# An attention and expert-layer kernel on one core: one wait of SyncE removed, three weight loads and two statistics steps moved in the order

## The chip, the cores and the metric

The kernel runs on one core of one Trainium2 chip. The metric is the device time of one execution in microseconds (us). The time before is the median of three runs.

## The reference, cut to what matters

```
x = x + xattn(layernorm(x), ctx, mask, mask, Wq, bq, Wk, bk, Wv, bv)   # 8 batches of 256 x 512, 16 heads
n = layernorm(x)                                                      # the last axis, 512 long
shared = (sigmoid(flat @ shared_gate.T) * (flat @ shared_up.T)) @ shared_down.T   # flat: 2048 rows of n
comb   = the two largest of softmax(flat @ router_w.T) over 8 experts, 0 elsewhere
he     = sigmoid(flat_bf16 @ w_gate[e].T) * (flat_bf16 @ w_up[e].T)               # 352 wide
routed = sum over e of comb[:, e] * (he @ w_down[e].T)
x = x + (n + shared + routed)
```

The change touches the passage from the attention part to the expert part: the end of the attention sum, the second layernorm, the shared gate and up products, and the loads of the expert weights.

## The kernel before, in words

Each of the five engines has a queue of its own (`Queue`, line 42). Every piece of work is put there with a number, its place, by `pe.at`, `act.at`, `dve.at`, `pool.at` or `sp.at`, and the queue is sorted by that number. So the numbers set only the order of the work of one engine. What one engine needs from another is a semaphore wait inside the piece, and everything behind a waiting piece on the same engine waits too. Two units of place matter: `base` is 17.0, where the attention units end, and `dt_` is 1/32, one step of the list `seq` (line 1179) of the shared part.

**The attention.** 16 units (two per batch) of 8 heads each are worked through. At the end of a unit `finish_unit` (line 1098) divides the result by the sums of the softmax: SyncE (SP) writes the reciprocals to DRAM (line 1128), reads them back spread over the partitions into `RB` (`gather_back`, line 1135, semaphore `rb`), and GpSimd (POOL) multiplies and adds to X (`add`, lines 1143 and 1144, semaphore `a`). The last unit is u = 15.

**The second layernorm.** It is done for four blocks of 512 rows: `norm(8)` to `norm(11)` (line 399). The statistics of the last block, `norm(11)`, are on VectorE (DVE): `first_three` (line 403) takes three of the four tiles and is placed 2.9 steps ahead of `stage_a` (line 420), which takes the fourth tile (line 429, it waits for `a` = 16) and closes the sums (line 431). `stage_p` (line 434, lines 440 to 449, nine small operations) turns them into scale and offset on POOL. ScalarE (ACT, `normalise`, line 482) then writes two normalised tiles of the block and DVE (`other_half`, line 492) the other two, both into Y[1].

**The shared products.** TensorE (PE) follows `seq`: ("T", blk, j) transposes half of a block (line 1259), ("G", blk, it) makes one third of gate and up (24 matmuls and more, line 1303), ("R", blk) turns the router's columns (line 1372), C and I work out and invert the places of the routed rows. T of block 3 waits for the two normalised halves (`xn` = 12 and `xd`). After each T, ACT or DVE takes the upper half of the number (line 1279) and DVE the lower one (`rest`, line 1284). After each G there is a chain ACT `tanh` (line 1325), DVE `hidden` (line 1338), ACT `upper` (line 1355), POOL `lower` (line 1360, semaphore `h`). From the third G on, `tanh` waits until `lower` of the G two places earlier is done.

**The normalised rows.** POOL writes a bf16 copy of each block (`narrow`, line 1621), and SP stores it to DRAM (`store_rows`, line 1629) into `yr`, from which the experts' rows are gathered later (line 1699, issued by POOL). The stores of blocks 0 and 2 count on `s_yr[0]`, those of blocks 1 and 3 on `s_yr[1]`. The store of block 0 first waits for `rb` = 256, the landing of the last `gather_back`.

**The expert weights.** 1088 KB for each of 8 experts go by POOL's own DMA queue into BIG (`load_expert`, line 332, the DMA at line 334). Their order and their waits are in `early_expert` (line 1658). Expert 0 is loaded early. Experts 1 and 2 stand at 16.95 and 16.951. Experts 7, 6 and 5 stand at `when(("G", 1, 2)) + .91 * dt_`, which is between `stage_p` of norm(11) (.90) and `lower` of G(1, 2) (.92). All three wait for the end of the attention (`av`), expert 7 also for `fr0` and `fr1`, and expert 5 also for `s_yr[1]` = 16, the landing of the store of block 1, because it overwrites the copy that this store reads. The first expert product (line 1764) waits for all eight.

The order on POOL before, at the place in question: `add` of unit 15; loads of experts 1 and 2; `lower` of G(0, 2); `stage_p` of norm(11); loads of experts 7, 6 and 5; `lower` of G(1, 2); `narrow` of block 2. The order on DVE before: `hidden` of G(0, 2); `first_three`; `hidden` of G(1, 2); `rest` of T(2, 0); `stage_a`; `rest` of T(2, 1); `hidden` of G(0, 0); `other_half`.

Of the kernel before, what the change touches and what calls it, by code (L numbers as in the profile page):

```python
# [14 lines left out]
T = 512  # L15
NU = 16
# [51 lines left out]
def xattn_moe(nc, x, ctx, mask, maskc, wqkv, bqk, bv, sg, su, sd, we, out):  # L68
# [10 lines left out]
    with stack:  # L79
# [170 lines left out]
        pe, act, dve, pool, sp = (Queue() for _ in range(5))  # L250
# [81 lines left out]
        def load_expert(i):  # L332
            def emit(e):
                e.dma_start(BIG[:, i, :], we[i]).then_inc(s["we"], 16)
            return emit
# [861 lines left out]
        base, dt_ = 17.0, 1 / 32  # L1197
# [9 lines left out]
        def when(item):  # L1207
            if item in early:
                return 15.15 + .22 * early.index(item)
            if item in last:  # L1210
                n = last.index(item)
                return tb + BETWEEN[n] + 1.7 if n < nb else tb + NP + 2.1 + n * 2.5
            if item == ("R", 3):
                return base + (seq.index(item) + 1.2) * dt_
            if item == ("C",):
                return base + (seq.index(item) + 1.5) * dt_
            return base + seq.index(item) * dt_
# [405 lines left out]

        def store_rows(blk):
            def f(e):
                if blk == 0:
                    e.wait_ge(s["rb"], 16 * NU)
                e.wait_ge(s["yb"], blk + 1)
                e.dma_start(yr[512 * blk:512 * blk + 512].rearrange("(a p) t -> p a t", p=128), YBF[blk])\
                    .then_inc(s_yr[blk % 2], 16)  # L1630
            return f
# [15 lines left out]
        norm(8, 13.2, 13.3, (13.66, 13.85, 14.1, 14.3), (6.7, 7.7, 8.7, 9.7))  # L1647
        norm(9, 13.8, 13.85, (14.52, 14.68, 14.85, 15.02), (10.7, 11.18, 12.18, 13.18))
        norm(10, 15.04, 15.06, 15.72, (11.68, 12.68, 13.68, 15.02))
        norm(11, when(("T", 2, 1)) + .55 * dt_, when(("G", 1, 2)) + .9 * dt_, when(("G", 0, 0)) + .85 * dt_)  # L1650
        rows_at = (15.06, 15.4, when(("T", 2, 1)) + .9 * dt_, when(("T", 3, 1)) + .9 * dt_)
        for blk in range(4):
            pool.at(rows_at[blk], narrow(blk))
# [4 lines left out]
        def early_expert(i):  # L1658
            def f(e):

                if i == 0:
                    e.wait_ge(s_nl[1], 32 * 16)
                elif i <= 2:
                    e.wait_ge(s["rp"], zi["x", 31, 3, 1] + 1)
                if i == 7:
                    e.wait_ge(s["fr0"], NU)
                    e.wait_ge(s["fr1"], NU)
                if i == 3:
                    e.wait_ge(s["rc"], zi["k", 15, 1] + 1)
                    e.wait_ge(s["gu"], max(gi[q] for q in gi if q[1] == 1) + 1)  # L1670
                if i == 4:
                    e.wait_ge(s["gu"], max(gi[q] for q in gi if q[1] == 0) + 1)
                if i == 5:
                    e.wait_ge(s_yr[1], 16)
                if i >= 5:
                    e.wait_ge(s["av"], 4 * NG)
                load_expert(i)(e)
            return f
        pool.at(15.6, early_expert(0))
        for n, i in enumerate((1, 2, 7, 6, 5)):  # L1680
            pool.at(16.95 + n / 1000 if n < 2 else when(("G", 1, 2)) + (.91 + n / 1000) * dt_, early_expert(i))
        pool.at(when(("G", 3, 2)) + .3 * dt_, early_expert(4))
        pool.at(when(("G", 2, 0)) + .3 * dt_, early_expert(3))

# [300 lines left out]
```

## Time and profile before

| what | value |
|---|---|
| three runs | 655.5, 657.47, 662.83 us |
| median | 657.47 us |
| the profiled execution: its time | 655.5 us |
| the profiled execution: its span, first to last instruction | 653.6 us |
| mean granted TensorE clock, as a share of the full one | 0.995 |
| busy: PE, DVE, ACT, POOL | 606.2, 506.8, 472.1, 364.1 us |

The time is longer than the span by what lies around the instructions. A row of a timeline gives start, length, engine, line and operation; brackets at its end give the idle time of the engine before it and what ended that. SPq is SyncE's queue of DMA issues. A busy DMA share of 1.00 means that all 16 DMA engines of the core work.

### The profile page before, as it was taken

Reading aid. Unit: us, or ns where it says so; the run is one execution under the profiler, and the core shown is the slowest. Engines: PE = TensorE matmul, PEld = TensorE weight load, DVE = VectorE, ACT = ScalarE, POOL = GpSimd, SP = SyncE. Lnnn points to the kernel's source line nnn. Section 1 sums busy time; section 2 is a strip of 40 time slices with the busy share of each in tenths; the row PEclk is TensorE's granted clock in tenths of the full one; section 3 lists DMA queues with packets and bytes.
Section 4 is the critical chain, followed back from the end, with each engine's and each line's share of the span. In section 5 each row is a group of like instructions: output and inputs, shape, how many; then the busy total and the mean of one; then the engine's idle time right before and its main releaser. Section 6 shows DMA issues by size and latency. Waiting matters only on the chain.

```text
span 653.6 us, 12535 instructions
## 1 busy us (share of the span) xinstructions
PE 606.2 (93%) x4082; PEld 258.5 (40%) x4082; DVE 506.8 (78%) x982; ACT 472.1 (72%) x662; POOL 364.1 (56%) x497
## 2 busy tenths in 40 slices
PE   4799989999999999999999999889999889999987
PEld 4544333333333333333333232224554456666532
DVE  2489899999999999999999999855447634454577
ACT  3654999899899899899898879984432266667511
POOL 5558554684684684684684463051642577777510
PEclk9799999999999999999999999999999999999999
DMA  8642334544536436444343342124797323333278
GB/s 290 209 135 84 94 119 142 144 136 145 144 99 184 140 102 194 127 148 135 108 120 121 103 130 76 36 63 122 181 222 168 79 89 105 103 102 101 87 224 314
DMA packets 64990, 88.66 MB, mean 136 GB/s; under 512 B 12624, under 2 KB 45264, under 8 KB 63904
## 3 DMA queue, kind: packets, MB, share of 16 engines
q1 hardware_dynamic: 60032, 68.72, 34.5%
q0 software_dynamic: 4896, 19.14, 11.9%
q8 instruction: 35, 0.57, 0.4%
q14 instruction: 27, 0.22, 0.1%
HBM read 63.75 MB, written 32.74 MB: 148 GB/s over the span
## 4 chain that ended last, share of the span: by engine, by line
PE 71%; DVE 10%; issue 7%; ACT 5%; POOL 3%; DMA 2%; SPq 1%; ACTq 0%; POOLq 0%; DVEq 0%
PE PS L1080 17%; PE PS L983 11%; PE PS L1052 8%; DVE MX L993 7%; PE PS L1764 7%; PE PS L1303 6%; PE PS L842 5%; PE PS L1827 3%; PE PS L1575 3%; ACT E L1066 2%; PE PS L837 2%; PE PS L988 1%; PE PS L930 1%; POOL E L1360 1%; PE PS L1722 1%
## 5 line engine op out<-in xcount | busy, mean ns | idle before, releaser
L993 DVE TENSOR_REDUCE MX<-PS 128x1 f32<-128x512 f32 x512 | 323.0, 683 | 17.4 <-PE PS L983 15.4
L1066 ACT ACTIVATE E<-PS 128x1024 f32<-128x1024 f32 x256 | 253.5, 1020 | 32.7 <-PE PS L1052 28.6
L983 PE MATMUL PS<-BIG 53*128 53x512 f16 x512 | 128.6, 384 | 12.2 <-DVE MX L993 10.7
L1080 PE MATMUL PS<-E,BIG 128*32 128x512 f32 x1024 | 136.5, 605 | 2.0 <-ACT E L1066 2.0
L1052 PE MATMUL PS<-BIG 55*128 55x512 f16 x512 | 101.2, 381 | 8.2 <-ACT E L1066 3.5
L876 POOL TENSOR_TENSOR ML<-BIG,ML 128x512 f32<-128x512 f32 x30 | 38.3, 1276 | 102.8 <-ACT BIG L852 102.6
L983 PEld LDWEIGHTS PS<-BIG 53*128 53x128 f16 x512 | 34.4, 93 | 133.9 <-DVE MX L993 119.8
L1786 DVE SCALAR_TENSOR_TENSOR E<-WP,PS 128x352 bf16<-128x352 f32 x39 | 20.3, 521 | 51.8 <-ACT WP L1776 51.8
L852 ACT ACTIVATE BIG<-PS,BIG 128x256 f32<-128x256 f32 x64 | 35.7, 560 | 25.7 <-PE PS L837 14.3
L1764 PE MATMUL PS<-BIG,CT 128*128 x312 | 53.0, 313 | 0.6 <-issue 0.6
L1052 PEld LDWEIGHTS PS<-BIG 55*128 55x128 f16 x512 | 26.3, 94 | 49.1 <-ACT E L1066 19.4
L842 PE MATMUL PS<-BIG,TB 128*128 128x256 f16 x288 | 39.7, 274 | 0.3
L1813 ACT ACTIVATE XN<-PS 128x384 bf16<-128x384 bf16 x39 | 19.1, 490 | 27.0 <-PE PS L1802 26.0
L879 POOL TENSOR_TENSOR WP<-ML,WP 128x512 f16<-128x512 f32 x30 | 34.8, 1158 | 2.4
L1080 PEld LDWEIGHTS PS<-E,BIG 128*32 128x32 f32 x1024 | 20.2, 108 | 37.6 <-issue 28.0
L1764 PEld LDWEIGHTS PS<-BIG,CT 128*128 128x128 bf16 x312 | 29.0, 98 | 13.1 <-issue 1.3
L1303 PE MATMUL PS<-BIG,SW 128*128 128x512 f16 (+2 forms) x144 | 32.1, 380 | 0.6 <-DVE WP L1338 0.4
L842 PEld LDWEIGHTS PS<-BIG,TB 128*128 128x128 f16 x288 | 24.3, 98 | 20.7 <-ACT E L1066 10.7
L878 POOL TENSOR_TENSOR WP<-ML,zero 128x512 f16<-128x512 f32 x30 | 31.2, 1039 | 2.4
L1827 PE MATMUL PS<-BIG,XN 128*128 x117 | 31.6, 379 | 0.7 <-ACT XN L1813 0.7
L1303 PE MATMUL PS<-E,SW 128*128 128x512 f16 (+2 forms) x144 | 31.8, 379 | 0.0
L1143 POOL TENSOR_TENSOR ML<-ML 128x512 f32<-128x512 f32 x16 | 20.4, 1276 | 20.3 <-DMA ML<-scr_recs 20.3
(262 smaller groups left out, 924.0 us busy)
## 6 DMA issues: line engine op xcount, KB each, us to landing
scr_parts<-WP SPq DMA_DIRECT2D x96, 128.0 KB
BIG<-scr_parts SPq DMA_DIRECT2D x64, 192.0 KB
BIG<-in_we POOLq DMA_DIRECT2D x8, 1088.0 KB, 13.9
scr_u<-ML SPq DMA_DIRECT2D x32, 256.0 KB, 2.8
X<-in_x SPq DMA_DIRECT2D x8, 512.0 KB, 6.3
CT<-in_ctx SPq DMA_DIRECT2D x8, 512.0 KB, 4.2
ML<-scr_u SPq DMA_DIRECT2D x16, 256.0 KB
ML<-scr_recs SPq DMA_DIRECT2D x16, 256.0 KB
```

What stands on the lines that cost most here:

```text
L842: ins = e.matmul(PS[:, slot(name), 0:256], WH[:, i, a, kt, 128 * o:128 * o + 128], src[:, r, kt, cols], start=(kt == a == r == 0), stop=(k ...
L852: e.activation(FB[:, i, cols], PS[:, slot(name), 0:256], ACT.Identity, bias=COL[:, b % 2, 4 * i + 2 + o:4 * i + 3 + o], scale=COL[:, b % 2 ...
L876: e.tensor_tensor(t1, FB[:, i, :], MB[:, b % 2, :], ALU.mult).then_inc(fr, 1)
L879: e.tensor_tensor(PT[:, i, 1, :], t1, PT[:, i, 0, :], ALU.subtract).then_inc(pt, 1)
L983: e.matmul(PS[:, yi[name] % 3, :], QK[rows, qb(u), 0, j0 + jj, 128 * tt:128 * tt + 128], QK[rows, qb(u), 1, j0 + jj, :], start=True, stop= ...
L993: e.tensor_reduce(MX[:, g % 2, c:c + 1], PS[:, yi[name] % 3, :], AX.X, ALU.max)\
L1052: ins = e.matmul(PS[:, slot(name) + a, :], QK[rows, qb(u), 1, j0 + jj, 128 * st:128 * st + 128], QK[rows, qb(u), 0, j0 + jj, :], start=Tru ...
L1066: e.activation(E[:, st, 2 * jj:2 * jj + 2, :], PS[:, slot(name):slot(name) + 2, :], ACT.Exp, scale=1 / 1024).then_inc(s["rc"], 1)
L1080: ins = e.matmul(PS[32 * hh:32 * hh + 32, AVB, :], VT[:, b % 2, st, 4 * (g % 4) + hh, :], E[:, st, hh, :], start=(st == 0), stop=(st == 3))
L1303: ins = e.matmul(PS[0:wide, pair + c, :], wt[:, a, k, 128 * it:128 * it + wide], yT[blk][:, r, k, :], start=(k == 0 and a == r == 0), stop ...
L1764: ins = e.matmul(PS[:, 2 * a + c, 0:352], XT[j % 2][:, k, 128 * a:128 * a + 128], big[:, bass.ds(expert[q] + (1408 * c + 352 * k), 352)], ...
L1827: ins = e.matmul(PS[:, 4 + a, :], HT[j % 2][:, it, 128 * a:128 * a + 128], big[:, bass.ds(expert[r] + (2816 + 512 * it), 512)], start=(it ...
```

## The change

The first wait of the store of block 0 is taken out. `stage_a` of norm(11) moves back by 0.10 of a step, and `first_three` with it, from 17 + 1.65 steps to 17 + 1.75. The loads of experts 7, 6 and 5 move forward to 16.952 to 16.954, right behind those of experts 1 and 2.

```
         def store_rows(blk):
             def f(e):
-                if blk == 0:
-                    e.wait_ge(s["rb"], 16 * NU)
                 e.wait_ge(s["yb"], blk + 1)
...
-        norm(11, when(("T", 2, 1)) + .55 * dt_, when(("G", 1, 2)) + .9 * dt_, when(("G", 0, 0)) + .85 * dt_)
+        norm(11, when(("T", 2, 1)) + .65 * dt_, when(("G", 1, 2)) + .9 * dt_, when(("G", 0, 0)) + .85 * dt_)
...
         for n, i in enumerate((1, 2, 7, 6, 5)):
-            pool.at(16.95 + n / 1000 if n < 2 else when(("G", 1, 2)) + (.91 + n / 1000) * dt_, early_expert(i))
+            pool.at(16.95 + n / 1000, early_expert(i))
```

## Rows read from the trace of the kernel before

**Rows 1.** The page, busy time and share of the span by engine.
```profile
PE 606.2 (93%) x4082; PEld 258.5 (40%) x4082; DVE 506.8 (78%) x982; ACT 472.1 (72%) x662; POOL 364.1 (56%) x497
```

**Rows 2.** Waits of PE from 464 to 521 us: waiter, releaser, total, times, longest.
```profile
PE PS L1714 <- DMA CT<-scr_yr,IX: 1.6, 1, 1.6
PE PS L1510 <- DVE CT L1497: 0.3, 1, 0.3
```

**Rows 3.** Timeline of POOL, 440 to 532 us.
```profile
452.52 1.25 POOL L1143 TENSOR_TENSOR ML<-ML 128x512 f32<-128x512 f32 x1 [13.80 <-DMA ML<-scr_recs]
...
461.58 1.27 POOL L1143 TENSOR_TENSOR ML<-ML 128x512 f32<-128x512 f32 x1 [6.46 <-DMA ML<-scr_recs]
...
464.14 1.14 POOL L334 DMA_DIRECT2D BIG<-in_we  x2
465.29 1.17 POOL L1360 TENSOR_TENSOR ML<-WP,ML 96x512 f16<-96x512 f32 x1
466.54 0.23 POOL L440 TENSOR_SCALAR VE<-MV 128x4 f32<-128x4 f32 x1
...
469.88 1.72 POOL L334 DMA_DIRECT2D BIG<-in_we  x3
471.60 1.19 POOL L1360 TENSOR_TENSOR ML<-WP,ML 96x512 f16<-96x512 f32 x1
...
504.55 5.35 POOL L1360 TENSOR_TENSOR E<-WP,E 128x512 f16<-128x512 f32 x1 [0.33 <-ACT E L1355]
...
517.58 1.08 POOL L1699 DMA_INDIRECT CT<-scr_yr,IX  x1 [0.16 <-issue]
```

**Rows 4.** Timeline of all engines, 460 to 474 us.
```profile
463.52 1.23 DVE L1284 TENSOR_TENSOR E<-PS,E 128x1024 f16<-128x1024 f32 x1 [1.60 <-ACT E L1279]
...
464.66 0.68 DVE L429 BATCH_NORM_STATS2 ST<-X 128x6 f32<-128x512 f32 x1
...
467.37 0.69 ACT L1325 ACTIVATE WP<-PS,TB 128x512 f32<-128x512 f32 x1 [2.97 <-PE PS L1303]
...
469.84 1.52 ACT L482 ACTIVATE XN<-X,TB,RR 128x512 f32<-128x512 f32 x2 [0.40 <-POOL TB L449]
469.84 1.00 DVE L492 TENSOR_SCALAR XN<-X,RR,TB 128x512 f32<-128x512 f32 x2 [1.07 <-POOL TB L449]
...
472.82 1.36 PE L1259 MATMUL PS<-ident,XN 128*128 128x128 f32 x11
```

**Rows 5.** Timeline of DVE, 445 to 530 us.
```profile
456.36 2.14 DVE L407 BATCH_NORM_STATS2 ST<-X 128x6 f32<-128x512 f32 x3
...
504.46 4.42 DVE L1489 TENSOR_TENSOR XN<-bvB 128x4096 f16<-128x4096 f32 x1
```

**Rows 6.** Timeline of SP's DMA issues, 436 to 532 us.
```profile
448.37 0.58 SPq L1135 DMA_DIRECT2D ML<-scr_recs  x1
449.49 0.32 SPq L1095 DMA_DIRECT2D scr_u<-ML  x1
...
458.03 0.58 SPq L1135 DMA_DIRECT2D ML<-scr_recs  x1
461.53 0.38 SPq L1629 DMA_DIRECT2D scr_yr<-ML  x1
```

**Rows 7.** DMA issues (KB each, us to landing): stores of blocks 1 and 3, expert 1.
```profile
scr_yr<-BIG SPq DMA_DIRECT2D x1, 512.0 KB, 3.8
...
scr_yr<-E SPq DMA_DIRECT2D x1, 512.0 KB, 24.3
...
BIG<-in_we POOLq DMA_DIRECT2D x1, 1088.0 KB, 9.1
```

**Rows 8.** Windows of half a us (busy by engine, clock, DMA share, GB/s): the stores alone.
```profile
463.00:463.50 0.50, 0.50 (x5) 0.20 (x3) 0.00 (x0) 0.50 (x2) 0.50 (x1) 1.00 1.09 385
```

**Rows 9.** DMA queues from 483 to 485 us: packets, MB, share of 16 engines.
```profile
q0 software_dynamic: 44, 0.36, 84.8%
q1 hardware_dynamic: 48, 0.05, 8.7%
```

## The prediction

> **What bounds the kernel now.** The first view is the page: PE is busy for 93% of the span [rows 1], so a change elsewhere counts only where PE waits for it. The second view is the list of PE's own waits from 464 to 521 us, the stretch that the diff touches. It has two entries, 0.3 us for the lists of the routed rows and 1.6 us for the first gathered rows [rows 2]. So PE is the bound here, and whatever the diff does well can win at most 0.3 + 1.6 = 1.9 us in this stretch. None of the moved work stands in front of those two waits: one is for a DVE chain, the other for a gather that POOL issues at 517.58 us [rows 3]. Next come the timelines of the engines that feed PE, to see how late each feeding step may become. The tightest is the normalised block 3. ACT ends its half at 469.84 + 1.52 = 471.36 us and PE starts the transposes of that block at 472.82 us, without a wait [rows 4]. The slack is 1.46 us. Last come SP's issues and the DMA views, for what the removed wait held back.
>
> **The three loads, moved ahead on POOL.** Three issues take 1.72 us, and the two ahead of them 1.14 us, 0.57 each [rows 3]. Before, POOL ran: the two issues from 464.14, `lower` of G(0, 2) from 465.29, `stage_p` from 466.54 until ACT can start at 469.84 (3.3 us), and then the three issues up to 471.60 [rows 3, 4]. After, the same work in the new order is: five issues from 464.14 to 467.0, `lower` to 468.25, `stage_p` to 471.56. `lower` of G(1, 2) starts near 471.6 as before, since the three issues only changed sides; all later work of POOL is unmoved. Two things become 1.72 us late.
>
> The first is `lower` of G(0, 2), which releases `tanh` of G(0, 0). It ends at about 468.2 us where `tanh` began at 467.37 [rows 3, 4], so that becomes some 0.9 us late. Its `hidden` follows; PE needs it only for the second half of T(3), past 473 us, so this is covered. If the cover were gone it would cost that 0.9.
>
> The second is `stage_p`. The halves of block 3 are then ready at 469.84 + 1.72 + 1.52 = 473.08 us for ACT, and DVE's at 472.56. PE wants them at 472.82, so its slack of 1.46 turns into a wait of 0.26, with the semaphore 0.3 us. What is late next is PE itself: behind this wait stand T(3), R(2), G(0, 1) and all the rest of `seq`, and the PE list shows no idle place before the lists of the routed rows to absorb it [rows 2]. So 0.3 us goes to the end.
>
> The loads gain nothing by being early. The first product that needs them comes behind the first gather, issued at 517.58 us [rows 3], and the load that is last in the queue (expert 3) is not among them.
>
> **The moved statistics on DVE.** `first_three` (2.14 us [rows 5]) now comes behind `hidden` of G(1, 2), which ends near 461.9 us, so it fills 461.9 to 464.05. `rest` of T(2, 0) ran at 463.52 for 1.23 us [rows 4] and now runs to 465.3, about 0.5 us later. `rest` of T(2, 1) now comes ahead of `stage_a` and ends near 466.5; PE needs both for G(2, 2) at 467.6, so they are hidden with 1.1 us to spare. `stage_a` (0.68 and the closing sums, together 1.1 us) then ends near 467.6, where before it was done by 466.5. Its reader `stage_p` finds POOL busy until 468.25 anyway, and that is the cover: 0.65 us. Without it the move would cost what exceeds this. I take zero, with zero to 0.5 as bounds, the lateness of `rest`; nothing here can gain, because POOL and not DVE is what `stage_p` waits for.
>
> **The removed wait on SP.** The read-back of the last unit is issued at 458.03 and POOL takes its data at 461.58; the store of block 0 is issued at 461.53, as it lands [rows 3, 6]. Without the wait both stores (1 MB) are issued from about 458.6 on and move beside the read-back. That is the cost of this edit: the read-back feeds `add` of unit 15 and everything behind it on POOL, and since `stage_p` has no slack left, each tenth it is late is a tenth for PE. The trace has one neighbour. For unit 14 a store of 256 KB was issued 1.1 us behind the read-back: 448.37 to 452.52 is 4.15 us, against 3.55 for unit 15, which ran alone [rows 3, 6]. That is +0.6. The upper bound is that the whole of both stores goes ahead: 1.05 MB at 385 GB/s [rows 8] is 2.7 us. The lower bound is zero, for data that goes in the order of issue; it isn't below zero, as nothing of the read-back is issued earlier. I take 0.6, the nearest row. The gain of the edit, stores that land 3 us earlier, serves the load of expert 5, which now stands at 466.4 us and waits for the store of block 1. Issued at 459.1 and landing in 3.8 [rows 7], that store is done by 463.
>
> **A shared port.** POOL's `lower` at 504.55 took 5.35 us where others take about 1.17, and it began as DVE's 4.42 us comparison did [rows 3, 5]. After the change `other_half` on DVE (two operations, 1.00 us [rows 4]) starts at 471.6, together with POOL's next `lower`; before, it ran beside DMA issues. If DVE's second half of it had to wait for that `lower`, block 3 would be ready up to 1.2 us later, so zero to 1.2. I take zero, because either may come first and ACT's half ends 0.5 us after DVE's. The Trainium skill ("SBUF — State Buffer", section "SBUF: two separate sides") says that DVE and GpSimd share one port pair, that whichever starts first keeps it for its whole instruction, and that the other blocks. The row at 504.55 agrees; by the rule the sum would be higher by up to the 1.2 us just given, by its absence by none.
>
> **The sum.** 0.3 (stage_p) + 0.6 (read-back) + 0 + 0 = +0.9 us. On the profiled execution that is 655.5 + 0.9 = 656.4 us. This execution was 1.97 us below the median of the three runs, so against the median the forecast is 657.47 + 0.9 = 658.4 us. The bounds of the terms add up to +0.3 and to 0.3 + 2.7 + 0.5 + 1.2 = +4.7 us, that is 657.8 to 662.2. A measurement of this kernel can tell about 1%, 6.6 us, from no change, so I forecast no difference that can be told.
>
> **Rivals.** *A, the stores win outright.* The read-back lands 2.7 us late; PE waits 3.0 us at T(3), 660.5 us. For it: the DMA engines run at a share of 1.09 when the stores go [rows 8]. Against: the stores are issued behind it on the same queue. Still within 1%.
>
> *B, five loads are too many at once.* If POOL can't hand over the fifth before the first has landed, it stands there until 464.14 + 9.1 = 473.2 us [rows 3, 7]. Then follow the issue (0.57), `lower` (1.2), `stage_p` (3.3) and ACT (1.5): 479.8, where PE wanted 472.82. That is +7.0 us, 664.5, slower by 1.1%. It decides from the point where the number that may be under way is four. For it: no row shows five whole loads outstanding at once. Against: the fifth was issued at about 471.0 before, 6.9 us after the first and so before its landing at 9.1 us, and the three issues took no longer than 0.57 each. The trace thus nearly excludes it.
>
> *C, expert 5 waits for a slow store.* The store of block 3 took 24.3 us where that of block 1 took 3.8 [rows 7], because expert loads were under way: from 483 to 485 us the two queues moved nearly equal numbers of packets, 44 and 48, but 0.36 and 0.05 MB [rows 9]. If the store of block 1 met the loads like this, it would land at 459.1 + 24.3 = 483.4. POOL would stand until then, and block 3 would be ready at 490.0, 17 us late: 674.7 us, slower by 2.6%. It decides if the stores still have data to move when the loads' data starts, past 465 us. They end about 2 us before that, so it takes a read-back or a store that is later than any bound above. The Trainium skill ("DMA: Bandwidth & Descriptors", section "Queues, rings and completion order") says that each DMA engine takes turns between the queues by packet. Rows 9 agree, and it's the rule that speaks against putting this load forward.
>
> *D, a gain.* The early loads or stores free a DMA engine for something PE waits for. The PE list caps it at 1.9 us: 655.6 us. Against: both waits hang on work that the diff leaves alone. A gain beyond 1% has no place in the trace; what is left for it is the scatter of three runs (7.3 us).
>
> **How the numbers follow.** The forecast gets 0.73, A 0.10, B 0.03, C 0.03, D 0.08; 0.03 stays for a measured gain over 1% out of scatter. The range of the time is 655.3 to 662.5: from just below D to just above the sum of the upper bounds. Slower by over 1%: B and C and a little of A and of scatter, 0.07. Faster by over 1%: 0.03. Within 1%: 0.90.
>
> **What would show it.** POOL's timeline: five issues in a row of about 2.9 us, then `lower`, then `stage_p` about 1.7 us later than before, measured from the end of `add`. SP: the first `scr_yr` store right behind the last read-back, at about 458.6. POOL's line 1143 for unit 15 at 461.6 to 462.5. In PE's waits a new short one at line 1259 for block 3, 0.3 to 1.5 us, released by ACT 482 or DVE 492. The first expert product starts later by that much. It would be wrong if the fifth issue stands apart from the fourth (B or C), if PE's list shows no wait at 1259, or if the expert stage itself changed.

## The result

Over 20 runs each the changed kernel takes 664.47 us (median) and the kernel before 658.33 us. The ratio is 1.0094, with a 95% interval of 1.0076 to 1.0113, so the change costs 5.0 to 7.4 us. I had forecast +0.9 us and no difference that can be told, in a range up to 662.5 us. Twenty runs of each tell 0.2% apart, so the difference is clear of noise, and it lies outside the range. The forecast was wrong in size, and, as the rows show, in what PE would wait for.

The page of the changed kernel, its head:

```profile
span 662.2 us, 12534 instructions
PE 612.8 (93%) x4082; PEld 262.1 (40%) x4082; DVE 510.8 (77%) x982; ACT 472.6 (71%) x662; POOL 363.9 (55%) x497
```

DVE and PE became busier with the same instructions (506.8 and 606.2 us in [rows 1]): something takes longer, not only later. Not all of it is due to the change. Of PE's 6.6 us only 1.7 belong to the transposes told of below. Around the first gathered rows PE is 1.4 us busier at a granted clock of 0.86 instead of 1.00, yet the stretch is no longer (12.41 us, 12.42 before); p1_no_wait shows the same 0.86 there, p2_stats 1.00. The waits of PE from 464 to 530 us, which answer to [rows 2], name the place:

```profile
PE PS L1259 <- DVE XN L492: 3.6, 1, 3.6
PE PS L1712 <- DMA CT<-scr_yr,IX: 2.4, 2, 1.5
PE PS L1303 <- DVE WP L1338: 0.4, 1, 0.4
PE PS L1510 <- DVE CT L1497: 0.3, 1, 0.3
```

There is one new entry, the first. (The 0.4 us at line 1303 was there before too, 0.44 us at 461.97 us, just ahead of the window of [rows 2].) PE waits 3.6 us for block 3, at the place where it had 1.46 us to spare, and the releaser is DVE's half of it (line 492), not ACT's. The timelines of POOL, DVE, ACT and PE around it answer to [rows 3] and [rows 4]:

```profile
467.12 2.73 POOL L334 DMA_DIRECT2D BIG<-in_we  x5
469.87 1.17 POOL L1360 TENSOR_TENSOR ML<-WP,ML 96x512 f16<-96x512 f32 x1
471.12 0.23 POOL L440 TENSOR_SCALAR VE<-MV 128x4 f32<-128x4 f32 x1
...
474.35 1.15 POOL L1360 TENSOR_TENSOR ML<-WP,ML 96x512 f16<-96x512 f32 x1
474.42 1.52 ACT L482 ACTIVATE XN<-X,TB,RR 128x512 f32<-128x512 f32 x2 [1.19 <-POOL TB L449]
474.42 4.55 DVE L492 TENSOR_SCALAR XN<-X,RR,TB 128x512 f32<-128x512 f32 x2 [1.86 <-POOL TB L449]
475.45 1.88 POOL L1621 CAST ML<-CT 128x2048 bf16<-128x2048 f32 x1
...
477.31 1.37 POOL L1360 TENSOR_TENSOR WP<-WP 128x512 f16<-128x512 f32 x1
```

```profile
479.11 3.58 PE L1259 MATMUL PS<-ident,XN 128*128 128x128 f32 x16 [3.62 <-DVE XN L492]
```

The two operations of line 492 took 1.00 us before and take 4.55 us now. Their single lengths are in the view of that line:

```profile
L492 DVE TENSOR_SCALAR XN<-X,RR,TB x2: 1370/2315/3260, 474.4 to 477.6; 128x512 f32<-128x512 f32 x2
```

The first takes 3.26 us and the second, which starts at 477.6, takes 1.37. POOL's `lower` started at 474.35, 0.07 us ahead of the first; POOL's copy of block 2 follows it without a gap and ends at 475.45 + 1.88 = 477.33; the first DVE operation ends 0.35 us after that. The second ends at 478.97, 0.3 us after the end of POOL's third operation. ACT, which had the same work and the same start, was done in its usual 1.52 us.

The second part of the loss is in the last row: the 16 transposes took 3.58 us. In the kernel before they had taken 1.91:

```profile
472.82 1.91 PE L1259 MATMUL PS<-ident,XN 128*128 128x128 f32 x16
```

The windows of the changed kernel (busy time by engine, granted clock, DMA share, GB/s) tell why:

```profile
475.50:479.10 3.60, 0.00 (x0) 0.02 (x1) 3.60 (x3) 1.80 (x3) 3.18 (x2) 1.00 1.08 227
479.10:483.00 3.90, 3.89 (x21) 3.55 (x22) 1.38 (x2) 1.92 (x3) 2.69 (x2) 0.56 1.02 216
483.00:493.00 10.00, 10.00 (x48) 5.20 (x48) 2.22 (x3) 2.08 (x3) 2.04 (x3) 1.00 1.03 224
```

After 3.6 us without work PE gets a mean clock of 0.56 for 3.9 us, which is the lower of its two levels (1.2 GHz) for most of that time, and then the full one again.

Now the account, each part measured from the start of the first G, at 448.73 us before and 451.31 after. The first transpose of block 3 stands at 24.09 us before and 27.80 after: +3.7. The transposes take +1.7. From their start to the first gather it is 44.76 us before and 46.28 after, so nothing but these 1.7 was added, and 0.15 came back. From the first gather to the first expert product it is 4.41 and 4.47, and from there to the placing of the last rows 100.9 and 100.6. This makes 5.0 of the 6.1 us between the medians; the interval begins at 5.0. The rest of the 8.6 us by which these two spans differ lies ahead of the first G (2.6) and behind the placing of the last rows (1.0). Both stretches differ as much between executions of kernels that are the same there: over the kernel before, p1, p2, p3 and p4 the first G starts between 448.73 and 452.57 us, and the last stretch lasts 30.5 to 34.0 us.

### The profile page after: what moved, and what is told of

It reads as the page before. It is cut to its first block, busy times and chain, and to the rows that moved or that the text cites. A ratio compares the mean times of both kernels' runs of the same rounds, so it can differ in the third digit from the quotient of the medians.

```text
span 662.2 us, 12534 instructions
## 1 busy us (share of the span) xinstructions
PE 612.8 (93%) x4082; PEld 262.1 (40%) x4082; DVE 510.8 (77%) x982; ACT 472.6 (71%) x662; POOL 363.9 (55%) x497
## 4 chain that ended last, share of the span: by engine, by line
PE 70%; DVE 10%; issue 7%; ACT 5%; DMA 4%; POOL 4%; SPq 1%; POOLq 0%; ACTq 0%
PE PS L1080 17%; PE PS L983 11%; PE PS L1052 8%; PE PS L1762 7%; DVE MX L993 7%; PE PS L842 5%; PE PS L1575 4%; PE PS L1825 4%; PE PS L1303 3%; ACT E L1066 2%; PE PS L837 2%; PE PS L988 1%; PE PS L930 1%; PE PS L1720 1%; PE PS L1259 1%
```

## The experiments

Twelve runs, in three groups. The second group (p5 to p10) and the third (the names with q) ran on two other chips, where the kernel before takes 694.29 and 693.43 us; each ratio is against the kernel before on the same chip in the same group. Beside the ratios stand what the profiles show at the place in question: the two operations of line 492, PE's wait ahead of the transposes of block 3, and the length of these.

| run | ratio, 95% interval | line 492, us | PE waits, us | transposes, us |
|---|---|---|---|---|
| before | 1 | 1.00 | none | 1.91 |
| changed | 1.0094 (1.0076 to 1.0113) | 4.55 | 3.62 | 3.58 |
| p1_no_wait | 1.0036 (1.0002 to 1.0069) | 1.00 | none | 1.91 |
| p2_stats | 1.0001 (0.9984 to 1.0017) | 1.00 | none | 1.91 |
| p3_loads | 1.0070 (1.0047 to 1.0092) | 4.55 | 2.78 | 3.57 |
| p4_pool_waits | 1.0036 (1.0015 to 1.0057) | 1.00 | 0.51 | 1.94 |
| p5_loads_later | 1.0020 (0.9986 to 1.0055) | 4.95 | 1.46 | 1.94 |
| p6_warm | 1.0057 (1.0025 to 1.0089) | 4.56 | 0.31 | 1.94 |
| p7_wait_and_stats | 1.0003 (0.9967 to 1.0039) | 1.00 | none | 1.91 |
| p10_loads_pool_waits | 1.0001 (0.9968 to 1.0035) | 1.00 | none | 1.94 |
| q_after | 1.0085 (1.0053 to 1.0118) | 4.55 | 3.48 | 3.35 |
| q_pool_waits | 1.0025 (0.9993 to 1.0057) | 1.00 | 0.77 | 1.94 |
| q_loads_pool_waits | 1.0017 (0.9989 to 1.0044) | 1.00 | none | 1.94 |
| q_no_wait | 1.0015 (0.9988 to 1.0042) | 1.00 | none | 1.91 |

### The three parts alone

**p1_no_wait**, the removed wait alone:

```
-                if blk == 0:
-                    e.wait_ge(s["rb"], 16 * NU)
```

> Before, with SP's wait for the read-back removed and nothing else. Theory P (the DVE half of block 3 is held off by POOL's operations that follow each other without a gap, which needs the loads moved away from beside it): no PE wait at line 1259, the two DVE operations of line 492 together 1.0 us as before, time within 0.2% of before. Rival R (the stores hold up the read-back, and that is the loss): line 1143 of unit 15 starts 4.2 us or more after the read-back's issue instead of 3.55, and the time rises by most of the 6 us. What I expect: line 1143 some 0.6 us late, hidden in the slack of 1.46 us, 0.0%.

**p2_stats**, the moved statistics alone:

```
-        norm(11, when(("T", 2, 1)) + .55 * dt_, ...
+        norm(11, when(("T", 2, 1)) + .65 * dt_, ...
```

> Before, with only the statistics of norm(11) moved by 0.10 of a step. Theory P: stage_p starts up to 1.1 us later on POOL, the slack of 1.46 us at T(3) takes it, line 492 stays at 1.0 us because the three load issues still stand behind stage_p; time within 0.2%. Rival S (the statistics are what makes block 3 late): a PE wait at line 1259 of over 1 us and a time over 0.4% above before.

**p3_loads**, the moved loads alone:

```
-            pool.at(16.95 + n / 1000 if n < 2 else when(("G", 1, 2)) + (.91 + n / 1000) * dt_, early_expert(i))
+            pool.at(16.95 + n / 1000, early_expert(i))
```

> Before, with only the loads of experts 7, 6 and 5 moved forward; the wait of SP stays. Theory P: the whole loss is here. Line 492 takes 4 to 4.6 us for its two operations, PE waits 3.0 to 3.7 us at line 1259, the transposes behind it run at the lower clock, and the time is 0.7 to 1.0% above before. Rival Q (only the 1.72 us by which stage_p is late counts): PE waits about 0.3 us, line 492 takes 1.0 us, time within 0.1%. Rival R: close to before, since the stores don't meet the read-back.

The loads carry the loss. POOL, DVE and PE of p3_loads, in the same views as above:

```profile
465.39 2.73 POOL L334 DMA_DIRECT2D BIG<-in_we  x5
...
472.62 1.15 POOL L1360 TENSOR_TENSOR ML<-WP,ML 96x512 f16<-96x512 f32 x1
473.73 1.89 POOL L1621 CAST ML<-CT 128x2048 bf16<-128x2048 f32 x1
475.59 1.37 POOL L1360 TENSOR_TENSOR WP<-WP 128x512 f16<-128x512 f32 x1
```

```profile
472.69 4.55 DVE L492 TENSOR_SCALAR XN<-X,RR,TB 128x512 f32<-128x512 f32 x2 [1.87 <-POOL TB L449]
```

```profile
477.39 3.57 PE L1259 MATMUL PS<-ident,XN 128*128 128x128 f32 x16 [2.78 <-DVE XN L492]
```

Line 492 takes the same 4.55 us beside the same three POOL operations. PE waits 2.8 us, somewhat under the 3.0 expected. The statistics alone cost nothing: `stage_p` starts 18.67 us behind the first G instead of 17.81, it now waits for DVE, and the slack takes these 0.9 us. With the removed wait alone there is no wait of PE and line 492 stays at 1.00 us, as expected, but the ratio came out at 1.0036, not zero. The read-back of unit 15 took 4.41 us from issue to use (SP and POOL of p1_no_wait):

```profile
460.40 0.58 SPq L1135 DMA_DIRECT2D ML<-scr_recs  x1
461.03 0.46 SPq L1627 DMA_DIRECT2D scr_yr<-ML  x1
461.53 0.51 SPq L1627 DMA_DIRECT2D scr_yr<-BIG  x1
```

```profile
464.81 1.27 POOL L1143 TENSOR_TENSOR ML<-ML 128x512 f32<-128x512 f32 x1 [8.58 <-DMA ML<-scr_recs]
```

Over all profiles, those with SP's wait show 3.55, 3.53, 3.76, 3.44, 3.72 and 3.66 us for this way (before, p2, p3, p5, p10 and q_loads_pool_waits), and those without it 4.41, 4.15, 4.45, 4.40, 4.15, 4.12, 4.29 and 4.22 (p1, p4, p6, p7, q_after, q_pool_waits, q_no_wait and the changed kernel). So with the stores right behind it the read-back is 0.4 to 1.0 us late, around the 0.6 of the forecast. In the profiled execution of p1 this cost PE nothing: from the first G to the transposes of block 3 it is 24.08 us (24.09 before), and from there to the first gathered rows at PE 47.77 (47.79 before).

### The collision taken away

**p4_pool_waits** keeps the whole change, and lets POOL stand until DVE's half is written:

```
             def lower(e):
                 e.wait_ge(s["hi"], hq[item] + 1)
+                if item == ("G", 1, 2):
+                    e.wait_ge(s["xd"], 1)
```

> The changed kernel, with one wait added: POOL's lower of G(1, 2) waits for xd, so POOL touches nothing while DVE writes its half of block 3. All three parts of the change are in. Theory P: line 492 takes 1.0 us, PE waits 0.5 to 0.7 us at line 1259 (for ACT's half), the granted clock stays at its full level there, and the time comes back to 0 to 0.2% above before. Rival Q or R (lateness of stage_p or of the read-back): the time stays 0.7 to 1.0% above before, or gets worse by the 1 us that POOL stands.

```profile
473.18 1.00 DVE L492 TENSOR_SCALAR XN<-X,RR,TB 128x512 f32<-128x512 f32 x2 [1.86 <-POOL TB L449]
474.33 1.15 POOL L1362 TENSOR_TENSOR ML<-WP,ML 96x512 f16<-96x512 f32 x1 [1.18 <-DVE XN L492]
474.77 1.73 PEld L1259 LDWEIGHTS PS<-ident,XN 128*128 128x128 f32 x16 [0.95 <-issue]
474.80 1.94 PE L1259 MATMUL PS<-ident,XN 128*128 128x128 f32 x16 [0.51 <-ACT XN L482]
```

POOL standing idle for 1.18 us makes DVE's half 3.5 us shorter. The releaser is now ACT, the wait 0.51 us, the clock full. That is the state my forecast had described for the changed kernel. The ratio, 1.0036, is well below the 1.0094 and yet above the 0.2% that I had allowed.

**p5_loads_later** asks whether the collision does it even where `stage_p` is not late: the loads go back instead of forward.

```
-            ... else when(("G", 1, 2)) + (.91 + n / 1000) * dt_, early_expert(i))
+            ... else when(("T", 2, 1)) + (.92 + n / 1000) * dt_, early_expert(i))
```

> Before, with the loads of experts 7, 6 and 5 moved BACK, behind POOL's bf16 copy of block 2, instead of forward. stage_p is then not late at all (no issue is put ahead of it), but the two POOL operations that the issues kept away now follow it at once. Theory P (port): line 492 takes about 4.5 us, from 21.1 to 25.6 us behind the first G; PE, which wanted block 3 at 24.1, waits about 1.6 us, and with it possibly the clock of the transposes falls (up to 1.7 us more): 0.25 to 0.5% above before. Rival Q (lateness of stage_p by the issues ahead of it is the loss): no wait at line 1259, 0.0%, or a little better.

```profile
471.33 1.15 POOL L1360 TENSOR_TENSOR ML<-WP,ML 96x512 f16<-96x512 f32 x1
472.44 1.88 POOL L1621 CAST ML<-CT 128x2048 bf16<-128x2048 f32 x1
474.28 1.82 POOL L334 DMA_DIRECT2D BIG<-in_we  x3
```

```profile
471.40 4.95 DVE L492 TENSOR_SCALAR XN<-X,RR,TB 128x512 f32<-128x512 f32 x2 [0.57 <-POOL TB L449]
```

```profile
476.50 1.94 PE L1259 MATMUL PS<-ident,XN 128*128 128x128 f32 x16 [1.46 <-DVE XN L492]
```

None of the moved issues is ahead of `stage_p` here, and still DVE's half takes 4.95 us and PE waits 1.46. So the place of the loads between `stage_p` and the next POOL work was what protected DVE. The ratio itself, 1.0020 with an interval that holds 1, cannot confirm 1.5 us of 694; the rows do. The transposes behind this shorter wait kept the full clock.

### The second cost of PE's wait

**p6_warm** fills most of the wait with matmuls of no use, whose results the transposes overwrite.

```
                 wait_pair(e, item)
+                if item == ("T", 3, 0):
+                    for i in range(16):
+                        e.matmul(PS[:, pair, :], sgw[:, 0, 0, 0:128], yT[0][:, 0, 0, :], start=True, stop=True)
                 e.wait_ge(s["xn"], 8 + blk + 1)
```

> The changed kernel, with 16 matmuls of no use (128x512 fp16, some 0.22 us each, into the two banks that the transposes of block 3 overwrite) placed in PE's queue ahead of its wait for block 3. Theory C (PE's idleness costs a second time, by the lower clock of the transposes behind it): line 492 still takes 4.5 us and the transposes start as late as in the changed kernel, but they take 1.9 us instead of 3.6, granted clock 1.0, and the time falls by about 1.7 us, to 0.6 to 0.7% above before. Rival (the transposes are slow for another reason, such as their loads or the DMA traffic): they keep 3.6 us and the time stays at 0.9%.

```profile
475.99 3.62 PE L1256 MATMUL PS<-BIG,SW 128*128 128x512 f16 x16
479.92 1.94 PE L1262 MATMUL PS<-ident,XN 128*128 128x128 f32 x16 [0.31 <-DVE XN L492]
```

```profile
479.90:482.00 2.10, 2.08 (x20) 1.93 (x20) 0.47 (x1) 1.60 (x3) 0.89 (x1) 1.00 0.96 201
```

Line 492 still takes 4.56 us and the transposes start 27.95 us behind the first G, as late as in the changed kernel (27.80). But they take 1.94 us at a clock of 1.00. That PE had been idle is therefore what slowed them, and it costs 1.6 us. The time, 1.0057, is lower than q_after's 1.0085, but the two ran on different chips and their intervals overlap. So the runs don't show the gain in time by themselves; the length of the transposes and the clock do.

### What is left for the removed wait

**p7_wait_and_stats** is the changed kernel with the loads put back:

```
-            pool.at(16.95 + n / 1000, early_expert(i))
+            pool.at(16.95 + n / 1000 if n < 2 else when(("G", 1, 2)) + (.91 + n / 1000) * dt_, early_expert(i))
```

> The changed kernel without its moved loads: SP's wait removed and the statistics moved. Theory P: line 492 at 1.0 us, no wait of PE at line 1259 or one under 0.5 us (the read-back 0.6 late and the statistics 1.1 late now add up against a slack of 1.46), time 0 to 0.4% above before, as the removed wait alone was. Rival (the removed wait or the statistics carry the loss): 0.7% or more.

**p10_loads_pool_waits** is the kernel before with the loads moved forward and POOL's wait for `xd` (the edits of p3_loads and p4_pool_waits):

> Before, with the loads moved forward and POOL's lower of G(1, 2) waiting for xd; SP's wait and the statistics as before. If what was left in p4_pool_waits (0.36%) comes from the read-back that meets the stores, it's gone here: a PE wait of 0 to 0.3 us at line 1259 and a time within 0.15% of before. If it comes from the loads or from POOL's added wait, it stays at 0.3% or more.

Both came out at the time before, 1.0003 and 1.0001, each give or take some 0.35%. Without the loads the change costs nothing that can be seen; with the loads but without the collision (p10) neither. To set them side by side on one chip, four kernels were run together, of which q_after is the changed kernel without an edit, and the others repeat p4, p10 and p1.

> The changed kernel itself, beside three others on one chip, so that their differences can be told: 0.8 to 1.1% above before, with line 492 at 4.5 us, a PE wait of 2.8 to 3.7 us at line 1259 and the transposes behind it at 3.6 us.

> p4_pool_waits again: all of the change, with POOL's lower of G(1, 2) waiting for xd. Theory P alone: 0.1% above before (PE's 0.5 us wait). With a cost of the removed wait of its own, which would make the read-back late by a varying amount: 0.3 to 0.4%, and the same in q_no_wait.

> p10_loads_pool_waits again: SP's wait kept, statistics as before, loads forward, POOL waits for xd. 0.0 to 0.1% in either case; if it's 0.3% as q_pool_waits, the removed wait of SP isn't what separates them.

> p1_no_wait again: only SP's wait removed. 0.3 to 0.4% if the read-back that meets the stores costs something of its own in some executions; 0.0 to 0.1% if the 0.36% of the first time was scatter, as the slack of 1.46 us says.

On this chip the changed kernel costs 0.85% again, with the same wait, in PE's list of q_after:

```profile
PE PS L1259 <- DVE XN L492: 3.5, 1, 3.5
```

The other three lie at 0.15 to 0.25% with intervals that hold 1. q_loads_pool_waits, which keeps SP's wait, is not told apart from q_no_wait, which lacks it. So the 0.36% of p1_no_wait was not confirmed (0.15%, from -0.12 to 0.42), and p7, which lacks the wait too, had 0.03%. Whether the removed wait costs one or two tenths of a per cent in some executions, or nothing, stays open; it is not what makes the changed kernel slower.

## Why the prediction was wrong, by its own steps

**What bounds the kernel.** Right. PE at T(3) with 1.46 us of slack was the place, and the waits of PE behind it did not move.

**The three loads on POOL.** Right in its working. Five issues took 2.73 us (2.86 forecast). From the start of the X addition (line 1144) to that of `stage_p` it was 3.61 us and is 5.21, so +1.6 against the 1.72 of the forecast. `tanh` of G(0, 0) came 1.2 us late (0.9 forecast) and was covered. ACT's half was ready 24.6 us behind the first G where PE wanted it at 24.1. With the read-back's share in it this would have been a wait of some 0.5 us (0.9 forecast), and p4_pool_waits shows it as 0.51.

**The statistics.** Right, zero. **The removed wait.** The +0.6 us on the read-back was measured as 0.4 to 1.0.

**"A shared port": the step that failed.** I had seen the collision and named its two sides, and gave it zero, with an upper bound of 1.2 us. It made DVE's half 3.55 us longer, and 3.2 us of that reached PE. Three things were wrong in it. First, I bounded it by one POOL operation, the `lower` that starts with it. POOL had three operations in a row, and DVE's first operation did not come in between the first and the second of them. Second, I took the cost as what exceeds ACT's half by 0.5 us, where DVE's half came 3 us after ACT's. Third, I chose the value by the thought that "either may come first". It isn't open: POOL goes on from the last operation of `stage_p` to `lower` on its own, while DVE hears of it by a semaphore, and in the changed kernel, p3 and p5 POOL was ahead each time, by 0.07 us. The row at 504.55 [rows 3], 5.35 us for an operation of 1.17, had shown that one engine can hold the other for as long as it works. In the kernel before, the three load issues stood between `stage_p` and `lower` and kept POOL off for 1.72 us, which is longer than DVE needs.

The Trainium skill ("SBUF — State Buffer", section "Who interferes with whom") says that a DVE `tensor_scalar` can run in a mode that uses the port pair shared with GpSimd, and that whoever issues first keeps the pair while the other blocks fully. The rows agree, with 4.55 us against 1.00. What the runs show by themselves is that POOL's work at the same time holds DVE; that the port is the reason is the page's account. It speaks of the whole instruction of the other side; here one DVE operation waited through two.

**What the forecast lacked.** It took PE's wait at its own length. The wait of 3.6 us drew 1.7 us more from the transposes behind it, at the lower clock.

The sum with the measured terms is: 0.5 (stage_p and read-back, up to ACT's half), 3.2 more for DVE's half and its semaphore, 1.7 for the clock, 5.4 us in all, against 6.1 us (5.0 to 7.4) measured.

**The rivals.** A: the read-back was 0.4 to 1.0 us late, not 2.7. B: five issues took 2.73 us without a gap, so nothing was full. C: POOL didn't stand at the load of expert 5. D: no gain appeared. None of the four was what happened; the cause stood among the terms of the sum that I had put at zero.

None of the versions beats the kernel before. p10_loads_pool_waits equals it (1.0001 and, as q_loads_pool_waits, 1.0017); the earlier loads bring nothing, as expected, since nothing waits for them.

## What to carry to other kernels

When work moves on one engine, ask what the moved piece had kept apart, not only what it delays: here three DMA issues on POOL were the gap in which DVE could work. Where a VectorE operation like this `tensor_scalar` from SBUF to SBUF starts just behind GpSimd work, bound its cost by the whole row of GpSimd operations that follow each other without a gap. And where a wait of TensorE comes out at several us, add what the matmuls behind it cost at the lower clock.

## What the runs showed of the hardware

- A DVE operation of 0.54 us lasted 3.26 us beside two POOL operations of 1.15 and 1.88 us in a row, and the next one 1.37 us beside a third. POOL's third operation lasted 1.37 instead of 1.15 to 1.17 us, so a little went the other way. In p5_loads_later DVE's two operations lasted 3.51 and 1.52 us. The first ended 0.6 us after POOL's copy had, while POOL was already at its DMA issues, and the second overlapped those issues and the first 0.25 us of the `lower` behind them. In the kernel before both had lasted 0.54 beside such issues, where DVE had started first, by 0.04 us. Why the issues held DVE in the one case was not tried.
- It does not meet every DVE operation. The statistics of the changed kernel took their usual 2.14 us although POOL multiplied and added beside them:

```profile
464.35 2.14 DVE L407 BATCH_NORM_STATS2 ST<-X 128x6 f32<-128x512 f32 x3
```

```profile
464.56 1.27 POOL L1143 TENSOR_TENSOR ML<-ML 128x512 f32<-128x512 f32 x1 [7.00 <-DMA ML<-scr_recs]
465.91 1.27 POOL L1144 TENSOR_TENSOR X<-X,ML 128x512 f32<-128x512 f32 x1
```

- PE's clock: after 0.5, 0.8 and 1.46 us without work the 16 transposes took 1.94 us; after 2.78, 3.48 and 3.62 us they took 3.57, 3.35 and 3.58 us. In p3_loads the granted clock was 0.50 in the 2 us behind the wait:

```profile
477.40:479.40 2.00, 2.00 (x10) 2.00 (x11) 0.44 (x1) 0.67 (x2) 0.82 (x1) 0.50 1.02 212
```
